# Two stages made one in a four-block forward pass on Trainium2: the end of the second block, and the norm, queries, keys and values of the third

## The chip, the cores and the metric

The kernel runs on one core of one Trainium2 chip, in one launch. The metric is the device time in microseconds (us), as the median over the runs shown. Five engines work side by side and meet at semaphores: TensorE (PE), VectorE (DVE), ScalarE (ACT), GpSimd (POOL) and SyncE (SP, which here only issues DMAs). Matmuls write to PSUM; everything else that is named here lies in SBUF, but for the scratch tensors `Pd`, `Md` and `Acc1`, which lie in DRAM.

## The reference, cut to what the change touches

The network has four blocks. Each adds `s * silu(ffn)` to the residual `x`, and the next block starts from a layer norm of `x`. The third block's attention first norms its input once more. There are 4096 tokens of 128 channels.

```python
def _layernorm(x, axis=-1, eps=1e-05):
    m = jnp.mean(x, axis=axis, keepdims=True)
    v = jnp.var(x, axis=axis, keepdims=True)
    return (x - m) / jnp.sqrt(v + eps)
...
    x = x + s * g
    xn = _layernorm(x, axis=-1)
    s = _L2_attn_ref(xn, ...)
    g = _silu(_L2_ffn_ref(xn, ...))
...
        def _ln(x, g, b):
            m = jnp.mean(x, axis=-1, keepdims=True)
            v = jnp.var(x, axis=-1, keepdims=True)
            return (x - m) * jax.lax.rsqrt(v + LN_EPS) * g + b
...
            xn = _ln(x, g_attn, b_attn)
            qkv = (xn @ qkv_w + qkv_b).reshape(b, s, 3, H, HD)
```

So the third block needs two tensors: the plain norm of `x`, which its feed-forward part reads, and the norm of that norm with a gain and a shift, from which the queries, keys and values come. With v the variance of `x` and eps = 1e-5, the plain norm has mean 0 and variance v / (v + eps), so the second root can be had from the first variance: the two factors together are 1 / sqrt((1 + eps) v + eps eps).

## The kernel before

Activations lie with their 128 channels on the partitions and the 4096 tokens along the free dimension, and are worked on in 8 batches of 512 tokens. The residual is `X`, the norm `XN`; `SX` and `GX` are work tensors of the same size. A stage is one function with its own semaphores and buffers; at its end all engines meet at a barrier, and the semaphores are cleared. The order within a stage is written out by hand, engine by engine. Two stages matter here.

`close_phase` (called with the tag `c1`) ends the second block. SyncE loads the 8 batches of the feed-forward result (`acc`, 256 KB each) and then the weights of the third block. For each batch, in the order of the program, TensorE transposes it into `gps` (4 transposes, L1325), multiplies the attention's result with its output weights into `pps` (L1330), averages `X` over the channels into `mps` (the mean, L1336), and averages the squares into `vps` (the variance, L1317). A matmul of float32 with 512 columns is recorded as two. ScalarE takes the gate (Silu, L1347), the square (L1351), and then, each for all batches, Ln(variance + eps) (L1355) and Exp(-0.5 ...) (L1369), which together give the inverse root. VectorE makes the product with the gate (L1381), adds it to `X` (L1386), subtracts the mean into `XN` (L1375), and at the end multiplies `XN` by the inverse root (L1391). `gps` and `pps` have one PSUM bank each here, `vps` four.

`norm_and_split_phase` (tag `s2`; it is called again for the fourth block with the tag `s3`, which the change leaves as it is) computes the norm of `XN`: mean (L1985), centering into `SX` (L2070), square (L2020), variance (L1991), Ln (L2024), Exp (L2028). Then a loop over the batches. VectorE applies factor and gain (L2077) and the shift (L2080). TensorE makes queries and keys (L2008) and values (L2013). Each of queries and keys is split into three bfloat16 parts: ScalarE writes the high part (L2034), VectorE the rest (L2088), ScalarE the middle part (L2039) and GpSimd the low part (L2134, 128x512). SyncE stores the three parts to `Pd` (L2149). VectorE also adds the bias of the values into `VA` (L2101). The stage that follows, `maxima_and_mlp_phase`, first loads `Pd` back (L2165), and its feed-forward part reads `XN`.

The trace drops the numbers in buffer names: `c_gps` is `c1_gps`, `s_p` is `s2_p`, `w_w` are the weights in use.

## Time and profile before

| | us |
|---|---|
| median of 3 runs | 3060.95 |
| lowest and highest run | 3057.07, 3062.58 |
| the profiled execution's own time | 3063.14 |
| its span in the trace | 3061.4 |
| `close_phase`, from its first DMA to the first work of the next stage | 1268.27 to 1311.11 |
| `norm_and_split_phase` (`s2`), to the first work of the next stage | 1311.11 to 1368.73 |

The busy shares over the whole span are PE 81%, DVE 72%, ACT 56%, POOL 33%, but a stage has its own limits, and only the two stages above are touched. Times in the rows below are microseconds from the start of the span. The page's chain of work that ended last reaches back to 2717.95 only, so it does not cover these stages; they are read from the timeline, from the table of stretches and from the list of one line's instructions. In the timeline, instructions of one line that follow each other closely are merged into one row with their count; the number in brackets is the time for which the engine was idle before the row, and what ended it.

### The profile page before, as it was taken

Reading aid. Unit: us, or ns where it says so; the run is one execution under the profiler, and the core shown is the slowest. Engines: PE = TensorE matmul, PEld = TensorE weight load, DVE = VectorE, ACT = ScalarE, POOL = GpSimd, SP = SyncE. Lnnn points to the kernel's source line nnn. Section 1 sums busy time; section 2 is a strip of 40 time slices with the busy share of each in tenths; the row PEclk is TensorE's granted clock in tenths of the full one; section 3 lists DMA queues with packets and bytes.
Section 4 is the critical chain, followed back from the end, with each engine's and each line's share of the span. In section 5 each row is a group of like instructions: output and inputs, shape, how many; then the busy total and the mean of one; then the engine's idle time right before and its main releaser. Section 6 shows DMA issues by size and latency. Waiting matters only on the chain. (4 is left out here: it accounts for less than half of the span.)

```text
span 3061.4 us, 37648 instructions
## 1 busy us (share of the span) xinstructions
PE 2464.9 (81%) x10312; PEld 1075.7 (35%) x10312; DVE 2196.8 (72%) x6010; ACT 1701.7 (56%) x3079; POOL 1002.4 (33%) x971
## 2 busy tenths in 40 slices
PE   6666378875769999759999989967878888868887
PEld 2212266663343444323333333322331111224443
DVE  6999589994676655556565556668759999657776
ACT  3434344542646666452121128855569999777775
POOL 0222489981154544120000014400020000038886
PEclk8777566677879999889999999988988999989999
DMA  3112575515265665331010113300031111001110
GB/s 125 55 55 69 124 138 106 111 25 139 94 178 121 119 136 110 109 97 36 28 30 28 37 22 92 100 9 0 0 103 41 45 47 43 21 30 36 39 40 24
DMA packets 295846, 211.39 MB, mean 69 GB/s; under 512 B 155320, under 2 KB 263784, under 8 KB 295144
## 3 DMA queue, kind: packets, MB, share of 16 engines
...
## 5 line engine op out<-in xcount | busy, mean ns | idle before, releaser
L2997 ACT ACTIVATE ca_pw<-ca_ps,ca_mx 128x512 f32<-128x512 f32 x512 | 342.8, 929 | 9.8 <-DVE ca_mx L3033 9.7
L2871 DVE CUSTOM_DVE_ANT_0 mx_sums<-mx_ps,w_w2f 128x512 f32<-128x512 f32 (+3 forms) x512 | 220.4, 486 | 153.2 <-PE mx_ps L2849 153.2
L3033 DVE TENSOR_REDUCE ca_mx<-ca_ps 128x1 f32<-128x512 f32 x512 | 311.6, 679 | 1.5 <-PE ca_ps L2963 1.5
L2828 PE MATMUL gm_ps<-gm_h,w_w2f 128*128 128x512 f32 x512 | 245.4, 612 | 0.0
L2997 ACT ACTIVATION_READ_ACCUMULATOR ca_pw<-ca_ps,ca_mx 128x1 f32 x512 | 229.5, 448 | 0.0
L2963 PE MATMUL ca_ps<-qs,ks 128*128 128x512 bf16 x512 | 177.0, 399 | 49.3 <-ACT ca_pw L2997 31.7
L2559 ACT ACTIVATE ta_pw<-ta_ps,w_cst 128x1280 f32<-128x1280 f32 x128 | 168.0, 1322 | 35.3 <-PE ta_ps L2440 35.0
L2903 ACT ACTIVATE gm_h<-gm_ps,w_w2f 128x512 f32<-128x512 f32 x64 | 44.0, 688 | 253.1 <-PE gm_ps L2828 253.1
L2278 ACT ACTIVATE at_pw<-at_ps 128x1280 f32<-128x1280 f32 x128 | 154.8, 1236 | 28.0 <-PE at_ps L2243 28.0
L2698 DVE TENSOR_TENSOR ta_pw<-ta_pw,w_cst 128x384 f32<-128x384 f32 x128 | 70.8, 553 | 134.8 <-ACT ta_pw L2559 132.9
L2605 POOL DMA_INDIRECT Acc<-XN,f_idx x64 | 104.5, 1633 | 157.0 <-DVE XN L2669 142.4
L2292 POOL MEMSET at_qs<- 128x1024 uint32 x4 | 3.7, 954 | 448.3 <-POOLq L36 448.3
L2974 PE MATMUL ca_o<-ca_pw,ca_vs 128*32 128x512 f32 x1024 | 138.4, 616 | 2.1 <-POOL ca_vs L3008 2.1
L761 DVE TENSOR_REDUCE rs_st<-rs_run 128x32 f32<-128x128 f32 x512 | 122.0, 284 | 11.7 <-ACT XN L786 11.7
L2963 PEld LDWEIGHTS ca_ps<-qs,ks 128*128 128x128 bf16 x512 | 40.1, 97 | 252.5 <-ACT ca_pw L2997 215.7
L3008 POOL TENSOR_TENSOR ca_vs<-VA,ca_rz 128x64 f32<-128x64 f32 x64 | 19.0, 297 | 331.9 <-DVE ca_rz L3020 331.9
L2828 PEld LDWEIGHTS gm_ps<-gm_h,w_w2f 128*128 128x128 f32 x512 | 89.3, 189 | 91.7 <-issue 91.7
L2309 DVE TENSOR_TENSOR at_pw<-at_pw,w_cb_f 128x384 f32<-128x384 f32 x128 | 70.3, 555 | 65.6 <-ACT at_pw L2278 65.5
L659 PE MATMUL ex_hps<-ex_xgt,ex_w 128*128 128x128 f32 x384 | 68.3, 332 | 47.8 <-ACT ex_h L815 25.3
L744 DVE TENSOR_TENSOR rs_run<-rs_st,rs_lay 128x96 f32<-128x96 f32 x512 | 105.7, 248 | 0.4 <-DVE rs_st L761 0.3
L2849 PE MATMUL mx_ps<-mx_ks,mx_qs 48*128 48x512 bf16 (+3 forms) x512 | 93.8, 304 | 13.7 <-DMA mx_ks<-Pd 13.7
L2301 POOL TENSOR_SCALAR_AFFINE_SELECT at_pw<-at_pw 128x128 f32<-128x128 f32 x128 | 72.8, 570 | 94.8 <-ACT at_pw L2278 94.8
...
## 6 DMA issues: line engine op xcount, KB each, us to landing
...
```

Of the source, the lines that this page charges most:

```text
L744: v.tensor_tensor(rows(n, 0, 3, half)[:, :, :, :, 0], state(n - 1, half).unsqueeze(1).to_broadcast([128, 3, V4, N]), given(n, KK, 3), ALU. ...
L761: v.tensor_reduce(state(n, half).rearrange("p v k -> p (v k)"), rows(n, 2, 2, half).rearrange("p r v k s -> p (v k) r s"), AX.XY, ALU.add) ...
L2278: act.activation(pw[:, s % BUF, 0:SPAN], ps[:, s % 2, 0:SPAN], ACT.Exp, scale=float(1 / np.sqrt(D))).then_inc(S["power"], 1)
L2559: act.activation(pw[:, s % BUF, 0:SPAN], ps[:, s % 2, 0:SPAN], ACT.Square, scale=0.25 * 0.5 ** 0.5, bias=cst("rhalf")).then_inc(S["power"], 1)
L2605: g.indirect_dma_start(Acc, bass.IndirectOffsetOnAxis(ap=idx[:, u // 2, at:at + 1], axis=0), y[:, u % 2, c, :], None, compute_op=ALU.add). ...
L2828: last = pe.matmul(mps[:, f, :], W(("h1", "h2")[n - 2])[:, j * 512 + f * 128:j * 512 + (f + 1) * 128], src[:, j, :], start=(j == 0), stop= ...
L2849: last = pe.matmul(ps[:, u, at:at + n], qs[:, g, h % GH, jq * 128:(jq + 1) * 128], ks[:, g, h % GH, 0:n], start=True, stop=True)
L2871: last = v.tensor_tensor_reduce(out=sums[:, u, at:at + n], in0=ps[:, u, at:at + n], in1=K["w2f"]("down")[:, T - n:T], scale=-1.0, scalar=3 ...
L2963: pe.matmul(ps[:, q % BANKS, :], ks[:, G % 2, h % GH, jk * 128:(jk + 1) * 128], qs[:, G % 2, h % GH, :], start=True, stop=True).then_inc(S ...
L2974: last = pe.matmul(O[32 * a:32 * a + M, G % 2, :], vs[:, h % BUF, jk, :], pw[:, h % BUF, jk, :], start=False, stop=(a == GH - 1 and jk == ...
L2997: act.activation(pw[:, h % BUF, jk, :], ps[:, (h * NB + jk) % BANKS, :], ACT.Exp, bias=mx[:, h % H, jk:jk + 1], accum_out=z[:, h % H, jk:j ...
L3033: v.tensor_reduce(mx[:, h % H, jk:jk + 1], ps[:, q % BANKS, :], AX.X, ALU.max, negate=True).then_inc(S["top"], 1)
```

## The change

The two stages become one, `close_and_split_phase`. There is no barrier between them. The second norm's mean, centering, square, variance and Ln are gone. From each batch's variance ScalarE now takes two logarithms, one after the other: of (1 + eps) v + eps eps into `GX`, and of v + eps into `root`, which is the place of that batch's `acc` rows, and later two Exp: `inverse(t)` at the head of the batch's turn and `first_inverse(t)` at its end. VectorE's `normed` reads the centered `XN` and writes `SX`. The multiply that makes the plain norm, `XN * root`, which VectorE did for all batches in a row, is done by GpSimd, once per batch, behind the two low parts. `gps` and `pps` have two PSUM banks each, which later hold queries and keys; `vps` has two instead of four, and its bank is free for the next variance but one when the second logarithm has read it. Two variances stand between the first matmuls of later batches, instead of four; four squares stand between the gates instead of six.

```text
stage before                      stage after
c1: ... mean, variance, Ln        cs: ... mean, variance, Ln and Ln
    Exp x8, XN * root x8
barrier
s2: mean, centre, square,
    variance, Ln x8
    loop: Exp, gain, shift,           loop: Exp, gain, shift, products,
          products, split                   split, Exp, XN * root (GpSimd)
```

```diff
@@ -1279,118 +1279,6 @@
-def close_phase(nc, K, tag, Acc=None, w=None, loads=()):
...
@@ -2157,6 +2045,227 @@
+def close_and_split_phase(nc, K, first, loads):
...
+    H, D, N, PB = 16, 8, 2, 4
+    with ExitStack() as ctx:
...
+        mps = ctx.enter_context(nc.psum_tensor("cs_mps", [128, 2, T], F32))
+        ps = ctx.enter_context(nc.psum_tensor("cs_ps", [128, 2, N, T], F32))
+        vps = ctx.enter_context(nc.psum_tensor("cs_vps", [128, 2, T], F32))
+        acc = ctx.enter_context(nc.sbuf_tensor("cs_acc", [128, B, NB, C], F32))
...
+        def gps(b):
+            return ps[:, 0, b % 2, :]
+        def pps(b):
+            return ps[:, 1, b % 2, :]
+        def root(b):
+            return acc[:, b].rearrange("p j c -> p (j c)")
+        @block.sync
+        def _(sp):
+            for b in range(B):
+                sp.dma_start(acc[:, b], K["Acc1"].rearrange("(b j p) c -> b p j c", p=128, j=NB)[b]).then_inc(rows[b], 16)
...
+        @block.tensor
+        def _(pe):
+            def turned(b):
+                pe.wait_ge(rows[b], 16)
+                if b >= 2:
+                    pe.wait_ge(S["g"], b - 1)
+                for j in range(NB):
+                    last = pe.transpose(gps(b)[:, j * 128:(j + 1) * 128], acc[:, b, j, :], cst("ident"))
+                last.then_inc(S["gps"], 1)
+            def attended(b):
+                if b >= 2:
+                    pe.wait_ge(S["prod"], b - 1)
+                pe.matmul(pps(b), wo, SX[:, batch(b)], start=True, stop=True).then_inc(S["pps"], 1)
...
+            def variance(b):
+                pe.wait_ge(S["sq"], b + 1)
+                if b >= 2:
+                    pe.wait_ge(S["lnr"], b - 1)
+                pe.matmul(vps[:, b % 2, :], cst("mean"), GX[:, batch(b)], start=True, stop=True).then_inc(S["var"], 1)
+            turned(0)
+            attended(0)
+            turned(1)
+            attended(1)
+            for b in range(2, B):
+                turned(b)
+                attended(b)
+                mean(b - 2)
+                if b in (5, 6):
+                    variance(b - 5)
+            mean(B - 2)
+            variance(2)
+            mean(B - 1)
+            for b in range(3, B):
+                variance(b)
+            pe.wait_ge(F["first"], 16)
+            for b in range(B):
+                pe.wait_ge(S["xn"], b + 1)
+                for n in range(N):
+                    if b >= 2:
+                        pe.wait_ge(S["r"], N * (b - 2) + n + 1)
+                    pe.matmul(ps[:, b % 2, n, :], W("k" if n else "q"), SX[:, batch(b)],
+                              start=True, stop=True).then_inc(S["ps"], 1)
+                if b >= 2:
+                    pe.wait_ge(S["v"], b - 1)
+                for j in range(NB):
+                    last = pe.matmul(vps[:, b % 2, j * C:(j + 1) * C], SX[:, b * T + j * 128:b * T + (j + 1) * 128], W("v"),
+                                     start=True, stop=True)
+                last.then_inc(S["vps"], 1)
+        @block.scalar
+        def _(act):
...
+            def logs(b):
+                act.wait_ge(S["var"], b + 1)
+                act.activation(GX[:, batch(b)], vps[:, b % 2, :], ACT.Ln, bias=cst("eps_eps"), scale=1.0 + 1e-5).then_inc(S["ln"], 1)
+                act.activation(root(b), vps[:, b % 2, :], ACT.Ln, bias=cst("eps")).then_inc(S["lnr"], 1)
+            def inverse(b):
+                act.wait_ge(S["ln"], b + 1)
+                act.activation(GX[:, batch(b)], GX[:, batch(b)], ACT.Exp, scale=-0.5).then_inc(S["rstd"], 1)
+            def first_inverse(b):
+                act.wait_ge(S["lnr"], b + 1)
+                act.activation(root(b), root(b), ACT.Exp, scale=-0.5).then_inc(S["rstdr"], 1)
...
+            for b in range(B):
+                gate(b)
+                if b >= 4:
+                    square(b - 4)
+            for b in range(B):
+                logs(b)
+                if b < 4:
+                    square(b + 4)
+            for t in range(B + 2):
+                if t < B:
+                    inverse(t)
+                for n in range(N):
+                    if 1 <= t <= B:
+                        high(t - 1, n)
+                    if t >= 2:
+                        middle(t - 2, n)
+                if t < B:
+                    first_inverse(t)
+        @block.vector
+        def _(v):
...
+            def normed(b):
+                v.wait_ge(S["rstd"], b + 1)
+                v.scalar_tensor_tensor(out=SX[:, batch(b)], in0=XN[:, batch(b)], scalar=W("g_attn"), in1=GX[:, batch(b)],
+                                       op0=ALU.mult, op1=ALU.mult).then_inc(S["gained"], 1)
+                v.wait_ge(S["gained"], b + 1)
+                v.tensor_scalar(SX[:, batch(b)], SX[:, batch(b)], W("b_attn"), None, ALU.add).then_inc(S["xn"], 1)
...
+            for b in range(B):
...
+            centered(B - 2)
+            centered(B - 1)
+            v.memset(VA[:, :, :, D:D + 1], 1.0).then_inc(S["ones"], 1)
+            v.wait_ge(F["first"], 16)
+            for t in range(B + 1):
+                if t < B:
+                    normed(t)
+                if t:
+                    rest(t - 1, 0)
+                    rest(t - 1, 1)
+                    values(t - 1)
+        @block.gpsimd
+        def _(g):
+            for b in range(B):
+                for n in range(N):
+                    g.wait_ge(S["mid"], N * b + n + 1)
+                    g.tensor_tensor(p[:, b % PB, n, part_at(n, 2), :], r[:, b % 2, n, :], p[:, b % PB, n, part_at(n, 1), :],
+                                    ALU.subtract).then_inc(S["lo"], 1)
+                g.wait_ge(S["gained"], b + 1)
+                g.wait_ge(S["rstdr"], b + 1)
+                g.tensor_tensor(XN[:, batch(b)], XN[:, batch(b)], root(b), ALU.mult).then_inc(S["plain"], 1)
 
 
...
+        "eps_eps": np.full((128, 1), 1e-10, np.float32),
...
             own = [weights(layer, "w2"), weights(layer, "cb_f32")]
             branch = layer.enter_context(ExitStack())
-            close_phase(nc, K, "c1", K["Acc1"], K["w1"]("o"), own + [weights(branch, "w2f")])
+            own.append(weights(branch, "w2f"))
             scratch("Pd", [B, 2, 3, C, T], BF16)
             scratch("Md", [B, 2, 16, T], BF16)
-            norm_and_split_phase(nc, K, "s2", K["w2"], gain=K["w2"]("g_attn"), shift=K["w2"]("b_attn"), bias=K["w2"]("qk_b"))
+            close_and_split_phase(nc, K, own[0], own[1:])
```

How the instructions stand in a row is shown at three places. The first is ScalarE at the end of the norm. In the kernel before (L1355 is Ln, L1369 Exp, L2020 the square and L2024 the Ln of the second norm; the two branches are the seam between the stages):

```order
L1355 ACTIVATE GX<-c_vps,w_cst 128x512 x6
L1369 ACT_TABLE_LOAD
L1369 ACTIVATE GX<-GX 128x512 x8
L1287 UNCONDITIONAL_BRANCH
L2016 UNCONDITIONAL_BRANCH
L2020 ACTIVATE GX<-SX 128x512 x3
L2024 ACT_TABLE_LOAD
L2024 ACTIVATE GX<-s_ps,w_cst 128x512
```

In the kernel after (L2171 and L2172 are the two Ln, L2176 is `inverse`, L2180 `first_inverse`, L2186 the high part):

```order
L2171 ACTIVATE GX<-cs_vps,w_cst 128x512
L2172 ACTIVATE cs_acc<-cs_vps,w_cst 128x512
L2176 ACT_TABLE_LOAD
L2176 ACTIVATE GX<-GX 128x512
L2180 ACTIVATE cs_acc<-cs_acc 128x512
L2176 ACTIVATE GX<-GX 128x512
L2186 ACTIVATE cs_p<-cs_ps,w_w 128x512 x2
```

Eight Exp, the seam, and the second norm's squares and Ln no longer stand between the last Ln and the first Exp of the split, and there is one table load there where there were three; a second Ln stands behind each first, and a second Exp in each turn.

The second place is GpSimd. Before, from the end of the previous stage (ISA rows are the barrier and the clearing of semaphores, L2134 the low part):

```order
L2351 UNCONDITIONAL_BRANCH
L35 ISA x10
L2126 UNCONDITIONAL_BRANCH
L2134 TENSOR_TENSOR s_p<-s_r,s_p 128x512 x16
L1960 UNCONDITIONAL_BRANCH
```

After (L2263 is the low part, L2268 the plain norm; these two rows come 8 times each):

```order
L2460 UNCONDITIONAL_BRANCH
L35 ISA x7
L2258 UNCONDITIONAL_BRANCH
L2263 TENSOR_TENSOR cs_p<-cs_r,cs_p 128x512 x2
L2268 TENSOR_TENSOR XN<-XN,cs_acc 128x512
L2263 TENSOR_TENSOR cs_p<-cs_r,cs_p 128x512 x2
```

Behind each pair of low parts a multiply of 128x512 float32 stands now, and the pair of the next batch stands behind that.

The third place is TensorE in the fifth and sixth batch of the first half. Before (L1325 transposes, L1330 the attention's output, L1336 mean, L1317 variance):

```order
L1325 MATMUL c_gps<-w_cst,c_acc 128x128 x4
L1330 MATMUL c_pps<-SX,w_w 128x512
L1336 MATMUL c_mps<-X,w_cst 128x512
L1317 MATMUL c_vps<-GX,w_cst 128x512
L1325 MATMUL c_gps<-w_cst,c_acc 128x128 x4
```

After (L2109 transposes, L2115 the attention's output, L2121 mean, L2127 variance):

```order
L2109 MATMUL cs_ps<-w_cst,cs_acc 128x128 x4
L2115 MATMUL cs_ps<-SX,w_w 128x512
L2121 MATMUL cs_mps<-X,w_cst 128x512
L2109 MATMUL cs_ps<-w_cst,cs_acc 128x128 x4
L2115 MATMUL cs_ps<-SX,w_w 128x512
L2121 MATMUL cs_mps<-X,w_cst 128x512
L2127 MATMUL cs_vps<-GX,w_cst 128x512
```

The turn of the fifth batch holds no variance any more, so the transposes of the sixth follow its mean.

## Rows read from the trace of the kernel before

**Rows 1.** Stretches: from:to, us; busy us per engine; TensorE clock; DMA share; GB/s.
```profile
1279.00:1295.00 16.00, 15.65 (x52) 7.64 (x50) 11.51 (x18) 6.19 (x11) 0.00 (x0) 1.00 0.44 187
...
1311.11:1327.50 16.39, 15.61 (x32) 6.51 (x32) 6.00 (x9) 10.94 (x18) 0.00 (x0) 0.90 0.01 1
...
1341.72:1365.30 23.58, 14.37 (x60) 8.64 (x60) 19.57 (x26) 14.15 (x26) 15.25 (x13) 1.00 0.62 218
```

**Rows 2.** Timeline, TensorE, close stage: start, duration, instruction, [idle before it].
```profile
1288.46 0.60 PE L1325 MATMUL c_gps<-w_cst,c_acc 128*128 128x128 f32 x4
...
1288.90 1.02 PE L1330 MATMUL c_pps<-SX,w_w 128*128 128x512 f32 x2
...
1291.47 0.60 PE L1325 MATMUL c_gps<-w_cst,c_acc 128*128 128x128 f32 x4
```

**Rows 3.** Timeline, ScalarE, last gate to the first norm's table load.
```profile
1292.11 0.60 ACT L1347 ACTIVATE GX<-c_gps 128x512 f32<-128x512 f32 x1
...
1295.20 1.28 ACT L1355 ACT_TABLE_LOAD   x1
...
1297.08 0.62 ACT L1351 ACTIVATE GX<-XN 128x512 f32<-128x512 f32 x1
...
1297.60 0.68 ACT L1355 ACTIVATE GX<-c_vps,w_cst 128x512 f32<-128x512 f32 x1
...
1298.69 3.58 ACT L1355 ACTIVATE GX<-c_vps,w_cst 128x512 f32<-128x512 f32 x6
...
1302.29 1.28 ACT L1369 ACT_TABLE_LOAD   x1
```

**Rows 4.** Timeline across the seam, and ScalarE's second-norm table load.
```profile
1304.24 4.91 DVE L1391 TENSOR_TENSOR XN<-XN,GX 128x512 f32<-128x512 f32 x8 [7.22 <-ACT GX L1369]
...
1311.14 1.19 PE L1985 MATMUL s_mps<-XN,w_cst 128*128 128x512 f32 x1 [9.66 <-PEq L36]
...
1327.50 1.28 ACT L2028 ACT_TABLE_LOAD   x1
```

**Rows 5.** Timeline, split stage: clock after idling, then VectorE beside GpSimd.
```profile
1330.24 0.49 DVE L2080 TENSOR_SCALAR SX<-SX,w_w 128x512 f32<-128x512 f32 x1
...
1330.78 3.09 PE L2008 MATMUL s_ps<-SX,w_w 128*128 128x512 f32 x4 [4.03 <-DVE SX L2080]
...
1337.52 2.28 POOL L2134 TENSOR_TENSOR s_p<-s_r,s_p 128x512 bf16<-128x512 f32 x2 [84.55 <-ACT s_p L2039]
...
1337.78 1.88 PE L2008 MATMUL s_ps<-SX,w_w 128*128 128x512 f32 x4
...
1339.31 1.04 DVE L2077 SCALAR_TENSOR_TENSOR SX<-SX,w_w,GX 128x512 f32<-128x512 f32 x1
...
1344.17 2.45 POOL L2134 TENSOR_TENSOR s_p<-s_r,s_p 128x512 bf16<-128x512 f32 x2 [1.49 <-ACT s_p L2039]
1344.27 1.33 DVE L2080 TENSOR_SCALAR SX<-SX,w_w 128x512 f32<-128x512 f32 x1
...
1345.52 1.40 DVE L2088 SCALAR_TENSOR_TENSOR s_r<-s_ps,w_w,s_p 128x512 f32<-128x512 f32 x2
...
1346.82 0.69 ACT L2034 ACTIVATE s_p<-s_ps,w_w 128x512 bf16<-128x512 f32 x1 [1.11 <-PE s_ps L2008]
...
1347.44 0.74 DVE L2077 SCALAR_TENSOR_TENSOR SX<-SX,w_w,GX 128x512 f32<-128x512 f32 x1
```

**Rows 6.** Timeline, end of the split stage and start of the next.
```profile
1359.92 4.49 POOL L2134 TENSOR_TENSOR s_p<-s_r,s_p 128x512 bf16<-128x512 f32 x4 [1.49 <-ACT s_p L2039]
...
1368.73 0.35 SPq L2165 DMA_DIRECT2D mx_qs<-Pd  x1
```

**Rows 7.** One line's instructions (GpSimd, last stage): duration ns min/median/max.
```profile
L3441 POOL TENSOR_TENSOR ss_kq<-ss_t x64: 1259/1276/1728, 2740.9 to 3042.5; 128x512 f32<-128x512 f32 x64
```

**Rows 8.** Stretches of the stage that follows, columns as in rows 1.
```profile
1368.70:1420.00 51.30, 45.94 (x130) 17.91 (x131) 26.99 (x116) 10.09 (x13) 1.84 (x2) 0.90 0.27 54
1420.00:1700.00 280.00, 272.09 (x801) 106.78 (x800) 165.25 (x691) 54.83 (x72) 0.00 (x0) 0.98 0.10 30
```

161 lines of the change are left out of this document (64 added, 97 removed).

## The prediction

> **What bounds the kernel now.** I read the page first. VectorE and TensorE are busy 72% and 81% of the whole span, but that says nothing about the 100.5 us in which the two touched stages run, and the chain of work that ended last does not reach back to them. So I took the table of stretches for the two stages, then the timeline of each, engine by engine, looking for the engine with no idle time. There are four stretches, and the reader should see that each has another limit.
>
> In the close stage TensorE is full: 15.65 of 16.00 us at a granted clock of 1.00 [rows 1], and a batch takes 1291.47 - 1288.46 = 3.01 us from transposes to transposes [rows 2]: 0.44 for four transposes (1288.90 - 1288.46) and 0.86 for each of three matmuls. Then ScalarE is the limit: table load, Ln and squares from 1295.20 to 1302.29 without a gap, 0.58 a Ln (3.58 for six), 0.52 a square (1297.60 - 1297.08) [rows 3]. Then comes a serial part: Exp, VectorE's eight multiplies to 1304.24 + 4.91 = 1309.15, 1.99 us of seam until TensorE starts at 1311.14, and the second norm until the table load at 1327.50 [rows 4], TensorE busy 15.61 of 16.39 in it [rows 1]. Last is the split, where VectorE is the limit: its rows name no idle time, and a turn of one batch takes 3.94 us (GpSimd's 2.45 and its 1.49 of idle time): two rests and the values 1.92 (1347.44 - 1345.52), L2077 0.74, L2080 1.33 less small overlaps [rows 5].
>
> One row there matters most. L2080 takes 0.49 us while GpSimd is idle and 1.33 beside a running low part [rows 5]. GpSimd starts at 1344.17, two parts take 2.45, so the first ends about 1345.3, and L2080 ends at 1345.60, 0.3 later. L2077 at 1339.31 shows the same for an instruction with two SBUF inputs: it takes 1.04, and ends 0.55 after GpSimd's pair (1337.52 + 2.28 = 1339.80). GpSimd waits in turn: its pair takes 2.45 instead of 2.28. L2088, which reads PSUM, stays at its usual pace, 1.40 for two, though GpSimd runs beside it. So these engines take turns, instruction by instruction, where VectorE reads SBUF in these two forms. This agrees with the Trainium skill, SBUF — State Buffer, section Who interferes with whom: the pair of ports that the two share is a lock, held for the whole instruction, and a VectorE instruction with at most one SBUF input and outside the two-port modes does not contend.
>
> **Part 1, the first half.** Two variances stand before the last gate instead of four, so TensorE reaches it 2 x 0.86 = 1.72 us earlier, at 1292.11 - 1.72 = 1290.4 [rows 3]. Only one square stands behind that gate before the table load, so the load starts at 1290.4 + 2 x 0.52 = 1291.4 instead of 1295.20. From there ScalarE has the load (1.30), 16 Ln instead of 8 (16 x 0.58 = 9.28) and four squares (2.08): 12.7 us, to 1304.1. The moved variances lie beside it: one takes 1.02 [rows 2] beside two Ln of 1.16. That cover is thin, since `vps` has two banks and a variance waits for the second Ln of the batch two before; I add 0.1. At the lower clock a matmul takes 0.86 more, and it would show in the last three or four. The load ahead of the Exp comes at 1304.2, against 1302.29 before: **+1.9**. The two extra banks for `gps` and `pps` I cost at nothing, since TensorE was full with one.
>
> **Part 2, the serial part.** Everything between the two Exp loads goes: 1327.50 - 1302.29 = 25.21 us [rows 3, 4]: **-25.2**. It holds a table load and eight Exp with VectorE's multiplies behind them, the seam, and the second mean, centering, square, variance and Ln. What is late next is the gain and shift of the first batch, as it was. The weights of the third block are needed at 1306 and not at 1330. SyncE issues them behind the eight batches as before, and the DMA engines move only 187 GB/s from 1279 to 1295 and nothing to speak of after 1311 [rows 1], so I cost that wait at nothing.
>
> **Part 3, to GpSimd's first low part.** It came 1337.52 - 1327.50 = 10.02 us after the load [rows 4, 5]. Two more Exp are now ahead of it on ScalarE, in turns 0 and 1, of about 0.5 each; one lies in the wait for TensorE's first product. **+0.5**. The clock after the gap is in both kernels: TensorE idles 4.03 us and then takes 3.09 for what takes 1.88 at full clock [rows 5]. Now it idles some 4.5 us, so I leave it; it is worth 1.2 either way.
>
> **Part 4, from the first low part to the last.** Before, 1337.52 to 1359.92 + 4.49 = 1364.41: 26.9 us [rows 5, 6]. Now GpSimd has 16 low parts at 1.12 (4.49 for four) and, between first and last, 7 multiplies. Such a multiply isn't in these stages. The nearest row is L3441, 128x512 float32 in and out, 1.26 at least, 1.28 median and 1.73 at most [rows 7]; I take 1.25 from start to start, since nearly all of its 64 are at the low end. That is 17.9 + 8.8 = 26.7 us of GpSimd alone. To it come its waits for VectorE: 0.17 a pair as now, and about 0.43 for a multiply that meets L2077 (0.55 of port time less GpSimd's own start), in the five batches in which both loops run: 5 x 0.6 = 3.0. Sum 29.7: **+2.8**. VectorE's own turn gives the same: 1.92, L2077 0.82 (it waits for the second low part), L2080 1.36 (it waits for the multiply): 4.10 instead of 3.94. So the split becomes GpSimd's, hardly slower than before, and its last low part has the seventh multiply ahead of it. The eighth multiply is hidden under the last store: before, 1368.73 - 1364.41 = 4.32 us passed from the last low part to the next stage [rows 6], more than 1.3. ScalarE's extra Exp, 0.5 a turn, goes into its idle 1.11 for TensorE [rows 5].
>
> **Sum.** 1.9 - 25.2 + 0.5 + 2.8 = -20.0 us. On the profiled execution, 3063.14, this gives 3043.1 (a span of 3041.4); on the median of the runs shown, 2.2 lower, **3041.0**.
>
> **Bounds.** No waits between GpSimd and VectorE: only the seventh multiply's 1.25 is left of part 4: -21.6. The multiply at its dearest, 1.73: 7 x 0.45 = 3.2 more: -16.8. Clock not falling: 1.2 better. Clock low through the last variances: 4 x 0.4 = 1.6 worse. The three runs shown lie from 3.9 below to 1.6 above their median.
>
> **Rivals.** (a) *The port makes the multiply serial with VectorE.* For it: L2080 waits out a whole GpSimd instruction today, and a third one comes. Against it: 1.92 us of each VectorE turn read PSUM and do not take part. If the whole 1.25 is added to each turn, part 4 is 7 x 1.25 = 8.8 instead of 2.8: -14.0, **3047**. It shows as turns of 5.2 us. The Trainium skill, Perfetto Trace Analysis, section Optimizing Scalar/DVE Operations, warns just of this move: since the two share a read port, moving work between them might not help.
>
> (b) *The port costs nothing*, the multiply falls into the 1.49 us in which GpSimd waits for ScalarE in each turn today [rows 5]. Turns stay at 3.94: -21.6, **3039**. Against it: 1.25 plus starts is nearly all of that gap, and L2077 falls into it.
>
> (c) *The front comes no earlier.* If the gates stay at 3.01 us a batch and the load for Ln at 1295.2, as when a bank or a square holds the next gate, the second half starts 3.8 later: -16.2, **3045**. Against it: TensorE was 98% busy there.
>
> (d) *Slower, by the clock in the stage that follows.* There TensorE is busy 45.94 of 51.30 us and 272.09 of 280.00, at granted clocks of 0.90 and 0.98 [rows 8]: it is bound by TensorE. If that stage met another history of gaps and stayed at 1.2 GHz for 40 us more, 20 us would be lost and the gain gone; to be slower by over 0.2% needs 52 us more at the lower level. Today only about a tenth and then a fiftieth of the clock is missing, in spite of the same idle stretch ahead of it, which the change leaves. Price at 55 us: +7.5, **3068**.
>
> (e) *The merge does not do what it says.* The order of instructions shows that it does: one load ahead of the Exp, no second mean.
>
> **How the numbers follow.** Forecast 0.64 (3037.5 to 3044), (a) 0.12, (b) 0.12, (c) 0.07, (d) 0.02, and 0.03 for a gain that is mostly eaten by several of these at once. The range takes in (b) with a clock that does not fall and a low run, and (a) but for its last half us: 3035 to 3047.5. A change of 0.2%, 6.1 us, is about what a measurement of this kernel can tell from none. Forecast, (a), (b) and (c) are all faster by more: 0.95; within 0.2%: 0.03; slower: 0.02.
>
> **What would show it.** In the profile after: the load ahead of Ln near 1291.4 and the one ahead of Exp near 1304.2 (part 1, or (c)); the first low part some 10.5 later (part 3); turns of 4.1 us with GpSimd hardly idle, the gain at 0.8, the shift at 1.35 and multiplies of 1.3 to 1.7 (part 4), against 5.2 for (a) and 3.94 for (b); the last low part near 1344.4 and the next stage's first load near 1348.7, 20 earlier. All stages behind should be shifted by the same 20 us; if not, it is (d). The forecast is wrong at its root if the Exp load comes after 1308, or if weights or stores hold TensorE or ScalarE in the split.

## The result and the profile after

| | before | after |
|---|---|---|
| median, us | 3061.32 (4 runs, 3057.07 to 3062.58) | 3038.41 (4 runs, 3032.47 to 3040.84) |
| ratio after / before | | 0.9925, 95% interval 0.9907 to 0.9942 |
| span of the profiled execution, us | 3061.4 | 3036.0 |
| granted TensorE clock over the span | 0.884 | 0.884 |

The change is 22.9 us faster (3061.32 - 3038.41). Of the 25.4 us between the two profiled spans, 20.09 lie in the touched stages: from their first DMA to the first work of the next stage they took 1368.73 - 1268.27 = 100.46 before and 1345.80 - 1265.43 = 80.37 after. The stages ahead were 2.84 shorter and those behind 2.47. The experiments show how far these two scatter with the same code there.

The table of stretches of the kernel after comes first: from:to, us; then busy us of TensorE, weight loads, VectorE, ScalarE and GpSimd; TensorE's clock; DMA share; GB/s.

```profile
1276.00:1286.90 10.90, 10.90 (x39) 5.57 (x38) 8.40 (x14) 4.50 (x9) 0.00 (x0) 1.00 0.71 302
1286.90:1304.70 17.80, 9.97 (x20) 3.40 (x19) 5.95 (x10) 15.78 (x26) 0.00 (x0) 0.94 0.00 0
1311.37:1340.96 29.59, 17.40 (x76) 10.52 (x75) 23.89 (x31) 21.45 (x39) 29.59 (x24) 0.99 0.53 188
1345.80:1400.00 54.20, 48.50 (x138) 18.99 (x139) 27.82 (x119) 10.13 (x13) 1.84 (x2) 0.89 0.27 51
```

There are three limits where there were four. TensorE is busy for 10.90 of 10.90 us while the batches come in. Then ScalarE is, between its two table loads. Once the loop of the split has filled, GpSimd is, for 29.59 of 29.59 us, 24 instructions without a gap. The serial stretch of [rows 4] is gone.

The next rows are the timeline of ScalarE (L2163 gate, L2167 square, L2171 first Ln, L2176 `inverse`) and of TensorE's first query and key products (L2150): start, duration, instruction, idle time before it.

```profile
1285.79 0.60 ACT L2163 ACTIVATE GX<-cs_ps 128x512 f32<-128x512 f32 x1 [1.90 <-PE cs_ps L2109]
1286.28 0.62 ACT L2167 ACTIVATE GX<-XN 128x512 f32<-128x512 f32 x1
1286.92 1.28 ACT L2171 ACT_TABLE_LOAD   x1
...
1299.90 1.28 ACT L2176 ACT_TABLE_LOAD   x1
...
1303.36 3.75 PE L2150 MATMUL cs_ps<-SX,w_w 128*128 128x512 f32 x4 [4.78 <-DVE SX L2223]
```

Between the last gate and the load for Ln stands one square; in [rows 3] 3.09 us lay between them (1295.20 - 1292.11), here 1.13. The second load comes 12.98 us after the first, and it is the last before the split. TensorE's first products then take 3.75 us after 4.78 of idle time, against 3.09 after 4.03 in [rows 5].

Then two turns of the split on VectorE (L2220 gain, L2223 shift, L2229 rests) and GpSimd (L2263 low parts, L2268 the plain norm's multiply).

```profile
1317.45 0.84 DVE L2220 SCALAR_TENSOR_TENSOR SX<-XN,w_w,GX 128x512 f32<-128x512 f32 x1
...
1317.70 1.71 POOL L2268 TENSOR_TENSOR XN<-XN,cs_acc 128x512 f32<-128x512 f32 x1
...
1318.32 1.37 DVE L2223 TENSOR_SCALAR SX<-SX,w_w 128x512 f32<-128x512 f32 x1
...
1319.38 2.46 POOL L2263 TENSOR_TENSOR cs_p<-cs_r,cs_p 128x512 bf16<-128x512 f32 x2
...
1319.62 1.40 DVE L2229 SCALAR_TENSOR_TENSOR cs_r<-cs_ps,w_w,cs_p 128x512 f32<-128x512 f32 x2
...
1321.79 1.71 POOL L2268 TENSOR_TENSOR XN<-XN,cs_acc 128x512 f32<-128x512 f32 x1
```

A turn takes 4.09 us (1321.79 - 1317.70). The gain meets the end of the low parts and takes 0.84; the multiply is held up by the gain and takes 1.71; the shift waits out the multiply, 1.37. Neither engine has a bracket with idle time. Last, the end of the stage on GpSimd and SyncE.

```profile
1337.52 1.26 POOL L2268 TENSOR_TENSOR XN<-XN,cs_acc 128x512 f32<-128x512 f32 x1
1338.74 2.26 POOL L2263 TENSOR_TENSOR cs_p<-cs_r,cs_p 128x512 bf16<-128x512 f32 x2
1340.96 1.26 POOL L2268 TENSOR_TENSOR XN<-XN,cs_acc 128x512 f32<-128x512 f32 x1
1345.80 0.34 SPq L2274 DMA_DIRECT2D mx_qs<-Pd  x1
```

VectorE is done here: the same multiply takes 1.26, and multiply and pair together 3.44 (1340.96 - 1337.52). So VectorE costs GpSimd 0.65 us a turn. The last multiply starts when the last low part has ended and lies under the last store.

### The profile page after: what moved, and what is told of

Its sections match the earlier page's. It is cut to its first block and busy times, and to the rows that moved or that the text cites. A ratio compares the mean times of both kernels' runs of the same rounds, so it can differ in the third digit from the quotient of the medians.

```text
span 3036.0 us, 37444 instructions
## 1 busy us (share of the span) xinstructions
PE 2432.3 (80%) x10189; PEld 1069.0 (35%) x10280; DVE 2186.8 (72%) x5994; ACT 1693.0 (56%) x3069; POOL 1013.6 (33%) x979
## 5 line engine op out<-in xcount | busy, mean ns | idle before, releaser
L3072 PE MATMUL ca_ps<-qs,ks 128*128 128x512 bf16 x482 | 167.2, 395 | 53.3 <-ACT ca_pw L3106 35.8
```

The lines of the kernel that those rows point to most:

```text
L3072: pe.matmul(ps[:, q % BANKS, :], ks[:, G % 2, h % GH, jk * 128:(jk + 1) * 128], qs[:, G % 2, h % GH, :], start=True, stop=True).then_inc(S ...
```

## The experiments

Each profiled execution was cut at the same marks. In the table they are counted from the stage's first DMA: the table load ahead of Ln, the load ahead of the split's first Exp, GpSimd's first low part, the end of its last one, and the first work of the next stage (before: the two stages together). "Behind" is the rest of the span. The ratio is to the runs of the kernel before in the same series; their median was 3061.32 for after, 3060.79 for after again, no multiply, multiply on VectorE and warm gap, 3058.51 for the last three rows, and 3062.31 for the others.

| kernel | Ln load | Exp load | first low | last low | next stage | behind | median, us | ratio to before |
|---|---|---|---|---|---|---|---|---|
| before | 26.93 | 59.23 | 69.25 | 96.14 | 100.46 | 1692.67 | 3061.32 | |
| after | 21.49 | 34.47 | 45.94 | 75.57 | 80.37 | 1690.20 | 3038.41 | 0.9925 (0.9907 to 0.9942) |
| after again | 21.36 | 34.33 | 45.77 | 75.39 | 80.18 | 1693.56 | 3038.15 | 0.9926 (0.9912 to 0.9939) |
| no multiply | 22.58 | 35.56 | 45.55 | 68.89 | 73.69 | 1688.28 | 3031.76 | one run |
| multiply on VectorE | 22.76 | 35.74 | 45.93 | 77.27 | 82.07 | 1696.04 | 3047.02 | one run |
| warm gap | 22.38 | 35.35 | 43.84 | 73.53 | 78.33 | 1690.41 | 3040.02 | 0.9936 (0.9921 to 0.9951) |
| seam | 22.44 | 36.00 | 45.84 | 75.54 | 80.34 | 1688.35 | 3042.21 | one run |
| one bank | 22.65 | 35.62 | 46.78 | 76.43 | 81.21 | 1688.85 | 3039.67 | one run |
| multiply spread | 22.45 | 35.43 | 45.60 | 73.72 | 79.55 | 1691.70 | 3048.09 | one run |
| spread and hold | 22.64 | 35.61 | 46.29 | 70.34 | 76.17 | 1693.00 | 3041.86 | 0.9930 (0.9912 to 0.9948) |
| best | 22.45 | 35.42 | 45.74 | 70.68 | 75.45 | 1685.88 | 3027.87 | 0.9893 (0.9877 to 0.9910) |
| best, warm start | 21.61 | 34.58 | 43.81 | 68.77 | 73.52 | 1687.94 | 3027.02 | 0.9901 (0.9883 to 0.9920) |
| before with hold | 27.09 | 59.23 | 69.33 | 93.36 | 97.69 | 1691.08 | 3054.51 | one run |

### The kernel after once more

No edit. It shows what the parts of the stage and the rest of the program do in another execution.

> The changed kernel once more, unaltered. The merged stage took 80.4 us from its first load to the next stage's first load in its first profile, against 100.5 for the two stages before, so 20.1 less, while the medians differ by 22.9 and the two profiled spans by 25.4: 2.8 us of that came ahead of the stage, where both kernels run the same code, and 2.5 behind it. Theory A (those are scatter between executions): the stage again 80.4 within 0.3, the start of the stage somewhere else between 1265 and 1269, and a ratio of the times between 0.992 and 0.994, that is 19 to 24 us. Theory B (the change reaches outside its stage, by the placing of instructions or buffers): the start of the stage again near 1265.4, 2.8 ahead, and a gain of 25 in the times.

Every mark is within 0.19 us of the first profile, while its span is 3043.0, 7.0 longer: the stages ahead took 3.83 more (the first DMA at 1269.26 against 1265.43) and those behind 3.36. In all the profiles of the table the first DMA lies between 1260.54 and 1275.15, and what is behind takes from 1685.88 to 1696.04, with no edit outside the stage but in the last kernel of the table. So only the marks can tell experiments apart that differ by one to six us, and of the 25.4 us between the two spans the 2.84 ahead and the 2.47 behind are within this scatter.

### Without the multiply

The disputed cost is taken away, and with it what it does to VectorE.

```diff
                                     ALU.subtract).then_inc(S["lo"], 1)
 
-                g.wait_ge(S["gained"], b + 1)
-                g.wait_ge(S["rstdr"], b + 1)
-                g.tensor_tensor(XN[:, batch(b)], XN[:, batch(b)], root(b), ALU.mult).then_inc(S["plain"], 1)
```

> The changed kernel without GpSimd's multiply for the plain norm; that part of the computation is left out, so the feed-forward part of the third block gets a centered tensor instead of a normed one. It prices the multiply. Port theory (the 2.7 us that the stretch from the first to the last low part grew are the multiply and its turns at the port with VectorE): the stretch falls from 29.6 to 26.9 or below, the gain and shift (scalar_tensor_tensor and tensor_scalar) go back to 0.75 and at most 1.33; the shift may even lose its wait if the low part no longer stands at the port when it comes, then turns of 3.2 to 3.4 and a stretch of 23.5 to 25. Rival (ScalarE's extra Exp makes the turn longer): turns stay at 4.09, the stretch loses only the last multiply, 28.3.

The stretch from the first to the last low part fell from 29.63 to 23.34 us, 3.55 below the kernel before, which has no multiply there either (26.89). A piece of its timeline, VectorE and GpSimd (line numbers as in after):

```profile
1319.72 0.49 DVE L2223 TENSOR_SCALAR SX<-SX,w_w 128x512 f32<-128x512 f32 x1
...
1320.04 2.31 POOL L2263 TENSOR_TENSOR cs_p<-cs_r,cs_p 128x512 bf16<-128x512 f32 x2 [0.90 <-ACT cs_p L2191]
...
1322.93 0.49 DVE L2223 TENSOR_SCALAR SX<-SX,w_w 128x512 f32<-128x512 f32 x1
...
1323.27 2.29 POOL L2263 TENSOR_TENSOR cs_p<-cs_r,cs_p 128x512 bf16<-128x512 f32 x2 [0.92 <-ACT cs_p L2191]
```

The turn is 3.21 us (1322.93 - 1319.72), and the shift takes 0.49 although GpSimd is as busy with low parts as in [rows 5], where it takes 1.33. The difference is who comes first. Here the shift starts 0.32 before GpSimd's pair; in [rows 5] GpSimd starts at 1344.17 and the shift at 1344.27, 0.10 behind it, and waits out a whole low part. Once a loop has fallen into one of the two orders it keeps it: GpSimd's lead is 0.11 to 0.15 in the last five shifts of before, and the shift's lead is 0.28 to 0.35 in the last six without the multiply. So the multiply's cost is 2.74 us against the kernel before, and 6.29 against the same kernel without it.

### The multiply on VectorE

The other place for the multiply: behind the values of each batch.

```diff
+            def plain(b):
+                v.wait_ge(S["rstdr"], b + 1)
+                v.tensor_tensor(XN[:, batch(b)], XN[:, batch(b)], root(b), ALU.mult).then_inc(S["plain"], 1)
...
                     values(t - 1)
+                    plain(t - 1)
...
         @block.gpsimd
...
-                g.wait_ge(S["gained"], b + 1)
-                g.wait_ge(S["rstdr"], b + 1)
-                g.tensor_tensor(XN[:, batch(b)], XN[:, batch(b)], root(b), ALU.mult).then_inc(S["plain"], 1)
```

> The changed kernel with the plain norm's multiply moved back to VectorE, inside the loop, behind the values of each batch. Port theory: VectorE is close to its limit and pays the multiply in full, 0.6 to 0.7 on its own and more where it waits for a low part: turns of 4.6 to 5.2, the stretch from first to last low part 33 to 36 us instead of 29.6, the stage 3 to 6 us longer than the changed kernel's. Rival (the port makes the multiply serial with VectorE wherever it runs, so GpSimd gains nothing over VectorE): turns of 4.1 to 4.2, the same as now, and the stage within 1 us.

The stretch is 31.34, 1.71 more than with the multiply on GpSimd. The direction was expected, the size was not: the loss is smaller than the 33 to 36 us that were expected. Its timeline, GpSimd (the low part is L2268 here) and VectorE:

```profile
1320.96 0.68 DVE L2240 TENSOR_TENSOR XN<-XN,cs_acc 128x512 f32<-128x512 f32 x1
...
1321.62 2.98 POOL L2268 TENSOR_TENSOR cs_p<-cs_r,cs_p 128x512 bf16<-128x512 f32 x2 [1.49 <-ACT cs_p L2191]
...
1322.33 1.26 DVE L2223 TENSOR_SCALAR SX<-SX,w_w 128x512 f32<-128x512 f32 x1
...
1326.09 2.99 POOL L2268 TENSOR_TENSOR cs_p<-cs_r,cs_p 128x512 bf16<-128x512 f32 x2 [1.49 <-ACT cs_p L2191]
```

The turn is 4.47 us (1326.09 - 1321.62): the 3.94 of the kernel before plus 0.53 for the multiply (L2240), which alone takes 0.68. The pair takes 2.98 instead of 2.46, and the shift again waits, 1.26. GpSimd idles 1.49 a turn as in [rows 5].

### Keeping TensorE busy in the gap

Five matmuls whose result nobody reads follow the last variance, so that TensorE idles less before the split.

```diff
             for b in range(3, B):
                 variance(b)
+            for _ in range(5):
+                pe.matmul(mps[:, 0, :], cst("mean"), X[:, batch(0)], start=True, stop=True)
             pe.wait_ge(F["first"], 16)
```

> The changed kernel with five idle float32 matmuls of 512 columns (means of the first batch into a PSUM buffer that nobody reads any more) on TensorE between the last variance and the wait for the first normed batch, where it idled 4.8 us. Theory (the first products ran at the lower clock because TensorE had idled: 3.75 us for what takes 1.88): the first product takes 1.9 and the first low part comes 2 to 3 us earlier, so the stage is 78 to 78.5 us instead of 80.4. Rival (the clock does not rise or hold by such work, or the added matmuls get in the way of the first product): the stage stays at 80.4 or is up to 1 us longer, and the first product still takes over 3 us.

The timeline of TensorE:

```profile
1301.23 4.45 PE L2145 MATMUL cs_mps<-X,w_cst 128*128 128x512 f32 x10
1306.17 1.96 PE L2152 MATMUL cs_ps<-SX,w_w 128*128 128x512 f32 x4 [0.49 <-DVE SX L2225]
```

The table of stretches, columns as above, over those first products:

```profile
1306.17:1308.13 1.96, 1.96 (x6) 1.00 (x7) 1.11 (x3) 0.69 (x1) 0.00 (x0) 1.00 0.03 8
```

The same stretch of the kernel after:

```profile
1303.36:1307.11 3.75, 3.75 (x5) 1.68 (x6) 1.75 (x3) 0.69 (x1) 0.00 (x0) 0.50 0.00 0
```

A granted clock of 0.50 is 1.2 GHz, 1.00 is 2.4 GHz. After 4.78 us without work the first products of after run at the lower level; after 0.49 us they run at the full one. From the Exp load to the first low part it took 8.49 us instead of 11.47. Against that profile of after the gap's price is thus 3.0 us and not the 1.2 of the prediction: the values' matmuls behind the first products are slow too. In the other profiles that keep the gap, the same distance is 9.84 to 11.44, and the first products take 3.41 to 3.75. So the price is 1.4 to 3.0 us, and it goes with how much of the full clock comes back behind the first products. Here are the 6.4 us from the first product on, in after and in the kernel of the next experiment:

```profile
1303.36:1309.76 6.40, 6.40 (x14) 3.71 (x15) 3.41 (x6) 2.41 (x4) 0.00 (x0) 0.53 0.01 3
1310.89:1317.29 6.40, 6.40 (x21) 3.64 (x22) 3.97 (x7) 3.54 (x7) 0.00 (x0) 0.76 0.01 3
```

The granted clock is 0.53 where the distance was 11.47, and 0.76 where it was 9.84. This agrees with the Trainium skill, TensorE: Matmul & The Clock Gate, part 1, which says that the number of slow matmuls differs between runs of one kernel. In the total time the 2 us are not resolved (0.9936, its interval overlaps that of after).

### With a seam

The stage is cut into two blocks at the Exp load, with a barrier between them; the norm itself stays as in after. The second half's code of each engine moves into the second block unchanged. It asks how much of the gain is the merge of the stages.

```diff
-        block = ctx.enter_context(nc.Block())
+        half = ExitStack()
+        block = half.enter_context(nc.Block())
...
+            v.wait_ge(F["first"], 16)
+
+        half.close()
+        nc.all_engine_barrier()
+        block = ctx.enter_context(nc.Block())
```

> The changed kernel with the merged stage cut again at the point where the old seam lay: behind the last Ln every engine meets at a barrier, and the split loop is a second block of code. The norm from the first variance stays. It tells apart the two halves of the 25.2 us that the prediction took away: the seam itself, and the second norm with the first norm's Exp and multiply. Theory (most of it is the norm; the seam costs its own time and nothing else): the load ahead of the Exp comes 1.5 to 2.5 us later, the stage takes 82 to 83 us instead of 80.3. Rival (merging the code is what pays, as engines would otherwise empty and refill over the seam): 5 us or more are given back, a stage of 85 or longer.

ScalarE's timeline at the cut (L2214 is `inverse`):

```profile
1306.32 0.68 ACT L2151 ACTIVATE cs_acc<-cs_vps,w_cst 128x512 f32<-128x512 f32 x1
1307.61 1.28 ACT L2214 ACT_TABLE_LOAD   x1 [0.60 <-PEq L2181]
```

From load to load it took 13.56 us where the others take 12.97 or 12.98: 0.6, not the 1.5 to 2.5 expected. The cut has a barrier but clears no semaphores, as the old seam of 1.99 us did [rows 4]. The stage as a whole took 80.34, not the 82 to 83 expected, but it can't show the 0.6: the clock behind the gap was higher than in after, and made the distance from the Exp load to the first low part 1.6 shorter (9.84 against 11.47). So, by the marks, most of the 25.2 us come from the arithmetic (no second mean, square and variance, no Exp in a row), and the merge as such has between 0.6 and 2.0 in it.

### One bank each for `gps` and `pps`

```diff
         def gps(b):
-            return ps[:, 0, b % 2, :]
+            return ps[:, 0, 0, :]
...
             def turned(b):
                 pe.wait_ge(rows[b], 16)
-                if b >= 2:
-                    pe.wait_ge(S["g"], b - 1)
+                if b:
+                    pe.wait_ge(S["g"], b)
```

`pps` is changed likewise.

> The changed kernel with one PSUM bank each for the transposed gate input and the attention's product, as before the change, instead of two. The prediction costed the second banks at nothing, since TensorE was full with one. Theory as predicted: the load ahead of Ln stays at 21.4 to 22.8 us from the start of the stage (the spread that four profiles show for the same code). Rival (with two variances fewer in a batch TensorE is no longer full, and the single bank would hold it at the gate or at the product): a batch takes 2.5 us or more instead of 2.15 from transposes to transposes, and the load comes 1 to 2.5 us later, at 23 to 25.

TensorE's timeline with one bank:

```profile
1275.53 0.60 PE L2109 MATMUL cs_ps<-w_cst,cs_acc 128*128 128x128 f32 x4
1276.56 1.12 PE L2115 MATMUL cs_ps<-SX,w_w 128*128 128x512 f32 x2 [0.42 <-DVE SX L2241]
...
1278.38 0.60 PE L2109 MATMUL cs_ps<-w_cst,cs_acc 128*128 128x128 f32 x4
...
1280.54 0.60 PE L2109 MATMUL cs_ps<-w_cst,cs_acc 128*128 128x128 f32 x4
```

The same place in after (third and fourth transposes), and the third product of the kernel before:

```profile
1272.66 0.60 PE L2109 MATMUL cs_ps<-w_cst,cs_acc 128*128 128x128 f32 x4
...
1274.81 0.60 PE L2109 MATMUL cs_ps<-w_cst,cs_acc 128*128 128x128 f32 x4
...
1277.60 1.13 PE L1330 MATMUL c_pps<-SX,w_w 128*128 128x512 f32 x2 [0.28 <-DVE SX L1381]
```

From the fourth batch on a batch takes 2.16 us, as in after. But the third takes 2.85 (1278.38 - 1275.53) where after has 2.15 (1274.81 - 1272.66), both at the full clock. TensorE waits there for VectorE (L2241), which has to empty the one bank of `pps`, and the kernel before has the same wait. From the first transposes to the fourth before took 8.44 us (1270.98 to 1279.42), and `spread_hold`, below, with two banks and nearly the same granted clock over the first 11 us (0.60 against 0.61), takes 7.65 (1274.41 to 1282.06). So the second banks are worth some 0.8 us, once, at the start of the stage. The mark does not show it: the load for Ln came at 22.65, within the 21.36 to 22.76 of all kernels with two banks, since the clock over the first 11 us was 0.68 here and 0.60 to 0.64 in those at 22.38 and later. The expectation, that this load would tell whether the banks matter, was too coarse.

### The multiply taken out of the split

GpSimd does the first two multiplies before its first low part, in time that it idles. VectorE does the other six when the last low part has ended.

```diff
                     values(t - 1)
+            v.wait_ge(S["lo"], N * B)
+            for b in range(2, B):
+                v.wait_ge(S["rstdr"], b + 1)
+                v.tensor_tensor(XN[:, batch(b)], XN[:, batch(b)], root(b), ALU.mult).then_inc(S["plain"], 1)
...
         def _(g):
+            for b in range(2):
+                g.wait_ge(S["gained"], b + 1)
+                g.wait_ge(S["rstdr"], b + 1)
+                g.tensor_tensor(XN[:, batch(b)], XN[:, batch(b)], root(b), ALU.mult).then_inc(S["plain"], 1)
```

> The changed kernel with the plain norm's eight multiplies put where their engines idle: the first two on GpSimd ahead of its first low part, the other six on VectorE behind the last low part, under the last store's landing. Leaving the multiply out gave turns of 3.21 us instead of 4.09. Two theories for that: (P) which comes first at the port, the shift or the low part, decides the turn, and with the multiply gone from the loop the shift comes first of itself, as in that run: turns of 3.2, a stretch of 23.5 us, a stage near 74.5; (Q) the order depends on how the first batches fall, and with two multiplies ahead of the first low part, it may land in the other order, as in the kernel before the change: turns of 3.9, a stretch of 27.5 to 28.5, a stage of 78.5 to 79.5. My layout says Q by a narrow margin.

GpSimd's timeline, and VectorE's row in it:

```profile
1324.69 2.45 POOL L2271 TENSOR_TENSOR cs_p<-cs_r,cs_p 128x512 bf16<-128x512 f32 x2 [1.49 <-ACT cs_p L2191]
...
1324.80 1.33 DVE L2223 TENSOR_SCALAR SX<-SX,w_w 128x512 f32<-128x512 f32 x1
...
1328.63 2.45 POOL L2271 TENSOR_TENSOR cs_p<-cs_r,cs_p 128x512 bf16<-128x512 f32 x2 [1.49 <-ACT cs_p L2191]
```

With no multiply in the loop the turn is 3.94 again, number for number that of [rows 5]: GpSimd starts 0.11 before the shift, and the shift waits. The other kernel without a multiply in the loop has turns of 3.21. So the order at the port, and not the amount of work, makes the difference. The six multiplies behind the split take 3.70 us on VectorE, and the next stage started 5.83 after the last low part instead of 4.80.

### The order at the port made fixed

To that kernel one wait is added: GpSimd starts a batch's low parts when VectorE has shifted the batch two ahead.

```diff
             for b in range(B):
+                if b + 2 < B:
+                    g.wait_ge(S["xn"], b + 3)
                 for n in range(N):
                     g.wait_ge(S["mid"], N * b + n + 1)
```

> As multiply_spread, and GpSimd holds the two low parts of a batch back until VectorE has done the shift of the batch two later, so that the shift never waits for a running low part. Theory (the port's order decides the turn): turns of 3.2 us whatever the first batches do, the shift at 0.49, a stretch from first to last low part of 24 us, a stage of 75 to 76 us, 4 to 5 less than the changed kernel; in the whole time a ratio to the kernel before of 0.990 to 0.992. Rival (the wait only moves the delay to GpSimd, and the rests then wait for the low parts): turns of 4 us and more, no gain.

GpSimd and VectorE in one turn:

```profile
1320.69 0.49 DVE L2223 TENSOR_SCALAR SX<-SX,w_w 128x512 f32<-128x512 f32 x1
...
1321.26 2.27 POOL L2273 TENSOR_TENSOR cs_p<-cs_r,cs_p 128x512 bf16<-128x512 f32 x2 [1.15 <-DVE SX L2223]
...
1324.68 2.28 POOL L2273 TENSOR_TENSOR cs_p<-cs_r,cs_p 128x512 bf16<-128x512 f32 x2 [1.15 <-DVE SX L2223]
```

A wait added to GpSimd makes the split faster: turns of 3.42, a shift of 0.49, and the stretch 24.05 where it was 28.12. The turns are 0.2 longer than the 3.2 expected. The releaser of GpSimd's idle time is now VectorE's shift and no longer ScalarE. In the total time the gain does not show (0.9930 against 0.9926 of after, where 0.990 to 0.992 was expected).

### The kernel before, with the same wait

The cleanest test of that reading: the old kernel, in which nothing but the order can change. The function also runs for the fourth block, behind the marks, and has the wait there too.

```diff
             for b in range(B):
+                if b + 2 < B:
+                    g.wait_ge(S["xn"], b + 3)
                 for n in range(N):
                     g.wait_ge(S["mid"], N * b + n + 1)
```

> The kernel before the change, and only the two low parts held back until the shift of the batch two later is done (in both stages that run this function). It tests the port's order in the old kernel, where a turn took 3.94 us with the shift at 1.33, and it is a second profile of the old close stage. Theory: turns of 3.2 us, the stretch from first to last low part 24 instead of 26.9, and the two stages together 97.5 to 98.5 instead of 100.5. Rival (in the old kernel VectorE is simply full, whatever the order): turns of 3.9, no change. For the old close stage: the load ahead of Ln again 26.9 from its start, within 1.4, and the load ahead of the second Exp 59.2 from there, within 1.5.

Its timeline, to be read against [rows 5]:

```profile
1339.54 0.49 DVE L2080 TENSOR_SCALAR SX<-SX,w_w 128x512 f32<-128x512 f32 x1
...
1340.10 2.28 POOL L2136 TENSOR_TENSOR s_p<-s_r,s_p 128x512 bf16<-128x512 f32 x2 [1.15 <-DVE SX L2080]
...
1343.53 2.27 POOL L2136 TENSOR_TENSOR s_p<-s_r,s_p 128x512 bf16<-128x512 f32 x2 [1.15 <-DVE SX L2080]
```

Turns of 3.43 instead of 3.94 (3.2 was expected), the shift at 0.49 instead of 1.33, the stretch 24.03 instead of 26.89, the two stages 97.69 instead of 100.46. The gain got dearer, 1.07 instead of 0.74, since it meets the low parts now, but the sum fell by 0.5 a turn.

### Everything together

`best` joins the spread multiplies, the wait on GpSimd and the matmuls in the gap, and lets VectorE do two of its six multiplies before the last low part. `best_warm_start` adds three more such matmuls ahead of `turned(0)`. The core of the edit of `best` on TensorE and VectorE; GpSimd's is that of the spread multiplies and the wait:

```diff
+            for _ in range(5):
+                pe.matmul(mps[:, 0, :], cst("mean"), X[:, batch(0)], start=True, stop=True)
             pe.wait_ge(F["first"], 16)
...
+            for b in range(2, B):
+                if b == 4:
+                    v.wait_ge(S["lo"], N * B)
+                v.wait_ge(S["rstdr"], b + 1)
+                v.tensor_tensor(XN[:, batch(b)], XN[:, batch(b)], root(b), ALU.mult).then_inc(S["plain"], 1)
```

> What the runs so far point to, together: the changed kernel with the five idle matmuls in TensorE's gap, the two low parts held back until the shift is done, two of the plain norm's multiplies on GpSimd ahead of its first low part, and six on VectorE behind its last values, four of them behind the last low part. Theory (the parts add up, since they lie in different stretches): spread_hold's 76.2 less 2.1 for the clock, less some tenths for the shorter tail: a stage of 73.5 to 74.3 us, so 26 to 27 us less than the kernel before's 100.5 and 6 to 7 less than the changed kernel's 80.3. Against the kernel before a ratio of 0.9895 to 0.992. Rival (the scatter of the rest of the program hides it, or something behind the stage gives it back): the stage as said, and a ratio no better than the changed kernel's 0.9926.

> As best, and three more idle matmuls on TensorE at the start of the stage, where it waits 2.7 us for the first batch from DRAM. The load ahead of Ln came 21.4 us after the start of the stage in the two profiles in which the granted clock of the first 11 us was 0.71 to 0.72, and 22.4 to 22.8 in those with 0.60 to 0.68. Theory (work in the wait brings the full clock earlier): a granted clock of 0.75 or more over the first 11 us and the load at 20.5 to 21.4. Rival (the clock rises when it rises, whatever these matmuls do, or they delay the first transposes): 22.4 or later.

Both stages are shorter than that of after, by 4.9 and 6.8 us. In `best` two things fell short, and the stage took 75.45 where 73.5 to 74.3 was expected; its timeline:

```profile
1304.91 1.59 DVE L2225 TENSOR_SCALAR SX<-SX,w_w 128x512 f32<-128x512 f32 x1
...
1304.96 1.26 POOL L2270 TENSOR_TENSOR XN<-XN,cs_acc 128x512 f32<-128x512 f32 x1 [53.76 <-DVE SX L2222]
...
1306.64 1.96 PE L2152 MATMUL cs_ps<-SX,w_w 128*128 128x512 f32 x4 [1.59 <-DVE SX L2225]
...
1331.96 5.38 POOL L2276 TENSOR_TENSOR cs_p<-cs_r,cs_p 128x512 bf16<-128x512 f32 x4
```

GpSimd's first multiply runs beside the very first shift, which takes 1.59 instead of 0.49 and delays the first product. And the last four low parts take 5.38 instead of the 4.49 of [rows 6], since VectorE's two early multiplies run beside them: what was moved out of the end came back in the split. In `best_warm_start` the same early multiply met the second gain instead (1.75 us), and the first product was not late. Its start, on TensorE:

```profile
1260.58 4.87 PE L2130 MATMUL cs_mps<-X,w_cst 128*128 128x512 f32 x6 [12.13 <-PEq L36]
1265.29 0.60 PE L2109 MATMUL cs_ps<-w_cst,cs_acc 128*128 128x128 f32 x4
```

Its first 11 us in the table of stretches:

```profile
1260.54:1271.54 11.00, 10.96 (x33) 5.69 (x34) 4.57 (x7) 3.67 (x5) 0.00 (x0) 0.81 0.93 301
```

The first transposes take 0.60, full speed, and the granted clock over the first 11 us is 0.81; the same stretch gives 0.62 in `best`, 0.71 in after and 0.61 in before. But the extra matmuls hold the first transposes back, from 2.8 us behind the first DMA to 4.75 (1265.29), so the load for Ln came at 21.61: 0.8 earlier than in `best`, not earlier than in after (21.49), and just outside the 20.5 to 21.4 expected. `best` is ahead of the changed kernel: 0.9893 (0.9877 to 0.9910) against 0.9925 and 0.9926, with intervals that hardly touch. `best_warm_start` is not told apart from `best` in total time. The median of `best` is 10.5 us below that of after. The kernel before was 2.8 lower in that series too, which leaves 7.7, more than the 4.9 of the stage; what is behind the stage took 1685.88 in its profile, the least of all, and no run shows why.

## Why the prediction was right

The time, 3038.41, lies in the range and 2.6 below the forecast of 3041.0. By its own steps, in us:

| step | predicted | measured |
|---|---|---|
| part 1, Exp load | +1.9 | +0.45 |
| part 2, serial part | -25.2 | -25.21 |
| part 3, to the first low part | +0.5 | +1.45 |
| part 4, first to last low part | +2.8 | +2.74 |
| from there to the next stage | 0 | +0.48 |
| sum | -20.0 | -20.09 |

The measured column is the difference of the two rows of the table of marks; part 2 is the distance 34.02 to 59.23 between the two Exp loads of before, as the prediction defined it, and part 1 is 34.47 - 34.02. The 22.9 of the medians and the 20.09 of the marks do not contradict each other: the interval of the ratio runs from 18 to 28 us.

**Part 1** had the right mechanism and one term wrong. The load for Ln came 5.44 earlier in this profile and 4.2 to 4.6 in the profiles of the experiments without extra matmuls ahead of the stage (a clock of 0.60 to 0.68 in the first 11 us, 0.61 in before), where 3.8 was predicted. At the clock of before, in `spread_hold` (0.60), the last gate came at 21.51 against 23.84: 2.3 instead of 1.72. The missing 0.6 is the second banks of `gps` and `pps`, which the prediction costed at nothing "since TensorE was full with one". It was full from 1279 on [rows 1]; in the first three batches it waited for the product. The second banks take 0.8 out there, less 0.17 by which the first transposes came later in that profile (2.88 behind the first DMA against 2.71). The profile of after had a clock of 0.71 in that stretch, which brought the rest of 5.44; no change of the kernel did. From load to load 12.98 was measured, 12.8 predicted. Rival (c) is out.

**Part 2** was read off and held. The wait for the weights, costed at nothing, does not show: the DMA share in the second stretch of after is 0.00, and what ends TensorE's idle time before the first products is VectorE's shift.

**Part 3** came out 1.0 dearer in this profile, by the clock. `multiply_on_vector` and `multiply_spread` have the granted clock of before over the 6.4 us from the first product on, 0.73, and take 10.19 and 10.17 from the Exp load to the first low part, against 10.02. So the extra Exp costs 0.15 and not 0.5, though TensorE idles 4.78 instead of 4.03. In after the clock in that stretch was 0.53, which cost another 1.3. "I leave it" was said of this clock, and "1.2 either way" was too little: the warm gap put the whole price at 1.4 to 3.0.

That the errors of parts 1 and 3 have opposite signs and nearly cancel is luck. The profile of after had a high clock at the front and a low one behind the gap; in `no_multiply`, the same code up to there, the load for Ln came 1.1 later and the first low part 1.5 sooner behind the Exp load.

**Part 4** was right to 0.1 in the sum and in each detail: turns of 4.09 (4.10), the gain 0.84 (0.82), the shift 1.37 (1.36), the multiply 1.26 alone (1.25) and 1.71 when it meets the gain. The model that carried it is that of two engines that take turns, instruction by instruction, where VectorE's gain and shift meet GpSimd; the rests, which read PSUM, keep to 1.40 for two beside it. The same lock is described in the Trainium skill, SBUF — State Buffer, section Who interferes with whom. Rival (a) would have given turns of 5.2, rival (b) 3.94. The Trainium skill, Perfetto Trace Analysis, section Optimizing Scalar/DVE Operations, says that moving work between these two engines might not help, and that was half right: the move to GpSimd is 1.7 us better in the stretch than the multiply on VectorE, and both are worse than taking it out of the loop.

But one statement of the prediction does not hold. It said that VectorE is the limit of the split at 3.94 us a turn, and counted the shift's 1.33 into that turn as given, though it had read it as a wait at the port. The wait depends on which engine starts first, GpSimd by 0.1 us or the shift by 0.3: the same loop runs at 3.43 in the old kernel with one wait more, and at 3.21 in the new one without the multiply. The sum did not suffer, because the change left the order as it was; had the multiply's absence or place turned the order, a prediction made from the durations of the one order would have missed by 3 us.

**The end.** The 4.32 from the last low part to the next stage were said to be unchanged, and were 4.80 in after and in eight of the other merged kernels to within 0.05; the two with six multiplies on VectorE behind the last low part have 5.83, the old kernel 4.33 with hold. So 0.48 belongs to the merged stage. The kernel without any multiply has it too, so it is not the eighth multiply. The clearing of the semaphores at the end of the stage, before and after (duration ns min/median/max, first and last start), shows what it is:

```profile
L35 POOLq EVENT_SEMAPHORE_RANGE_CLEAR  x3: 44/69/152, 1367.4 to 1368.3; - x3
L35 POOLq EVENT_SEMAPHORE_RANGE_CLEAR  x4: 45/69/157, 1344.0 to 1345.3; - x4
```

Semaphores are cleared group by group, with a barrier behind each. The merged stage has four groups where the old one had three, and the rounds follow each other in about 0.45 us (half of 1368.3 - 1367.4, and a third of 1345.3 - 1344.0 is 0.43).

**The clock downstream**, rival (d): after has 0.89 from 1345.80 to 1400.00, [rows 8] have 0.90, and the stages behind were not longer beyond their scatter of 10 us. The medians differ by 22.9, so nothing of the 20 us is seen to be lost.
